# Decoder of two layers: cross attention's last output product in two steps, its last maximum ahead of a division, and steps of five norms set elsewhere in VectorE's order

## The chip, the core and the metric

The kernel runs on one core of one Trainium2 chip. A core has five engines with instruction queues of their own: TensorE (PE, with its weight loads listed apart as PEld), VectorE (DVE), ScalarE (ACT), GpSimd (POOL) and SyncE (SP), which here only starts DMAs. They meet through semaphores. The metric is the device time of one execution in microseconds.

## The reference

The reference takes x (8 sequences of 112 tokens, 512 wide) and a context (8 x 375 x 512) through two pre-norm decoder layers, in float32:

```python
x = x + L0_attn(layernorm(x))                     # 32 query heads, 8 key heads, rotary, sinks
x = x + L0_xattn(layernorm(x), mask, ctx)         # 32 heads of 16; own keys, then gated context keys
x = x + L0_ffn(layernorm(x))                      # router, top 2 of 8 experts, gated GELU
x = x + L1_attn(layernorm(x))                     # causal, 16 query heads, low-rank keys and values
x = x + L1_xattn(layernorm(x), ctx, mask)         # one softmax readout of the context
x = x + L1_ffn(layernorm(x))                      # sigmoid/tanh waves, two blocks with combined weights
```

The masks come with the inputs. `layernorm` takes mean and variance over the 512 channels. In cross attention each head has one softmax over its own 112 keys and another over the 375 context keys; the context's is weighed with tanh of a gate.

## The kernel before

The tokens are 7 tiles of 128 rows (`x`, in SBUF all the time), and the attention stages go by 8 sequences of 112 rows in 4 pairs u. One list of steps, made by `build_order`, is walked by each engine, and each does its own share of a step in that order. A step early in the list is therefore early in every engine's queue that has a share in it, and a wait holds back all that follows on that engine. The functions that make the list merge a chain of attention steps with a row of filling steps: `spread` by costs, `cross` by costs and due times.

A norm of stage st and tile b is three steps. `stats` is VectorE's L1516 to L1520 (mean, variance, plus epsilon) and then GpSimd's power L2251, which gives `rstd`. `scale` is VectorE's L1529, which waits for `rstd`; in stage 0, from tile 4 on, GpSimd's share of `scale` is the addition L2256 of a bias to x. `turn` is TensorE's transposes L1053 and ScalarE's copy L2041. `norms(st, bs)` is all `stats`, then all `scale`.

Layer 0's attention, step by step for a sequence and a half of the heads: `s0` scores (L1100), `m0` maximum on VectorE (L1566) and exponentials on ScalarE, `d0` division on VectorE (L1578 to L1583) and GpSimd (L2271), `p0` transposes (L1109) with copies by ScalarE (even) and VectorE (odd, L1589), `v0` value products (L1119), `w0` output (L1131). The next pair's projections `kq0` (L1080, chunks of 8 matmuls) with their rotary ropes on VectorE (L1549 to L1553) and GpSimd (L2277, L2279) are the filling. A float32 matmul is two records in the trace.

Cross attention handles sequence b in four groups c of eight heads, each with two parities. For the context keys: `xc` scores (L1192), `cm` negative maxima (VectorE, L1634), `mt` turns the maxima on TensorE (L1199) and VectorE adds them to the queries (L1641), so that `xk` (L1209) gives shifted scores, `ce` takes ScalarE's exponentials (L2109), `xcv` is the context value product (L1239). `xu` copies numerator and denominator out of PSUM (ScalarE, L2121). `xd` is the division (VectorE L1649 to the reciprocal L1656; GpSimd L2320, L2325) and `xn` the normed value (L1664, L1666) with event `oxt`. `xw` t is the output product of tile t (L1247), four matmuls over c, and VectorE's addition to x (L1602). Tile 6 needs the last two sequences.

Behind it `ent` steps form the combined weights of layer 1's last stage (L1459, two matmuls of 512 columns each); they have nothing to do with the tokens and fill TensorE's time. Steps 0 to 11 run ahead of the experts. `route` (L1274), `lt` (L1284), VectorE's choice of two experts, `rank` (L1293 to L1296), GpSimd's scattering `put` (L2338), the loading of row blocks, `bt` (L1302) and `gu` (L1312) follow each other.

Layer 1's attention is like layer 0's: `s1`, `c1` 0 (mask addition, VectorE L1842), `c1` 1 (maximum L1848, L1850, and ScalarE's eight exponentials L2161), `p1` (copies L2169 and L1864), `v1` (L1414, copies L2175 and L1870), `w1` (L1426), `d1` (L1856, L1858). GpSimd adds a row to x with `bo1` (L2261).

## Time and profile before

| | us |
|---|---|
| median of 3 runs | 1756.43 |
| lowest and highest | 1752.63, 1756.64 |
| profiled execution, its own time | 1756.78 |
| its span | 1754.5 |
| TensorE busy | 1700.0 (97%) |
| VectorE busy | 986.4 (56%) |
| ScalarE busy | 548.0 (31%) |
| GpSimd busy | 458.5 (26%) |

The span goes from the first to the last recorded instruction; the time of the execution holds some 2.3 us more. The parts of this profile lie at these times: layer 0's attention to about 340 us, cross attention to 901, router and scattering to 946, experts to about 1190, layer 1's attention to about 1480, the readout and the last stage behind it.

### The profile page before, as it was taken

How to read it: one execution, taken by the hardware profiler on the slowest of the kernel's cores; microseconds unless marked ns; L12 is line 12 of the kernel's file. 1: busy time of each engine (PE TensorE's matmuls, PEld its weight loads, DVE VectorE, ACT ScalarE, POOL GpSimd, SP SyncE). 2: the span in 40 equal slices, each digit the busy share in tenths (PEclk: the TensorE clock that was granted, in tenths of full speed). 3: DMA queues.
4: the chain of work that ended last, by engine and by line, in shares of the span. 5: the costliest groups of instructions: out<-in, count | busy, mean ns of one | idle time of the engine just before them, and what ended most of it. 6: DMA issues, size and time to landing. Idle time of an engine off the chain costs nothing.

```text
span 1754.5 us, 32913 instructions
## 1 busy us (share of the span) xinstructions
PE 1700.0 (97%) x13868; PEld 1137.6 (65%) x13868; DVE 986.4 (56%) x1901; ACT 548.0 (31%) x1515; POOL 458.5 (26%) x549
## 2 busy tenths in 40 slices
PE   7999999999999999999999999998999999999998
PEld 6876666657666666666546888877677775444444
DVE  3765556437777777677743111116554555664987
ACT  0343333524444444445410111110422222333411
POOL 2532323512222213222113000005231210002676
PEclk9999999999999999999989999999999999999999
DMA  9100012000000000000147988866000033752101
GB/s 394 49 1 1 1 43 73 1 27 19 13 8 19 4 17 20 8 13 1 67 171 294 347 334 335 335 231 229 2 1 1 1 137 129 241 189 84 29 14 42
DMA packets 31987, 172.26 MB, mean 98 GB/s; under 512 B 4024, under 2 KB 4024, under 8 KB 18176
## 3 DMA queue, kind: packets, MB, share of 16 engines
q1 hardware_dynamic: 29600, 162.82, 24.9%
q0 software_dynamic: 2240, 7.34, 1.2%
q8 instruction: 109, 1.79, 0.4%
q14 instruction: 38, 0.31, 0.1%
HBM read 155.46 MB, written 16.52 MB: 98 GB/s over the span
## 4 chain that ended last, share of the span: by engine, by line
PE 86%; DVE 10%; POOL 1%; issue 1%; ACT 1%; DMA 1%; POOLq 0%; DVEq 0%; ACTq 0%
PE PS L1312 9%; PE PS L1080 7%; PE PS L1131 6%; PE PS L1381 5%; PE PS L1459 5%; PE PS L1169 5%; PE PS L1490 4%; PE PS L1321 4%; PE PS L1426 4%; PE PS L1192 3%; PE PS L1209 3%; PE PS L1477 3%; PE PS L1139 3%; PE PS L1156 2%; PE PS L1161 2%; DVE R L1618 2%
## 5 line engine op out<-in xcount | busy, mean ns | idle before, releaser
L1312 PEld LDWEIGHTS PS<-R,W 128*128 128x128 f32 x1344 | 153.2, 192 | 11.7 <-issue 11.7
L1312 PE MATMUL PS<-R,W 128*128 128x128 f32 x1344 | 153.6, 275 | 2.2 <-DVE R L1811 2.2
L1634 DVE TENSOR_REDUCE nmw<-PS 112x2 f32<-112x750 f32 x128 | 114.1, 934 | 42.5 <-PE PS L1192 42.5
L2251 POOL TENSOR_TENSOR rstd<-veps,mhalf 128x1 f32<-128x1 f32 (+1 forms) x71 | 53.8, 757 | 307.2 <-DVE veps L1520 284.0
L1080 PE MATMUL PS<-xT,W 128*128 128x224 f32 x640 | 127.8, 360 | 1.0 <-ACT xT L2041 0.7
L1080 PEld LDWEIGHTS PS<-xT,W 128*128 128x128 f32 x640 | 122.2, 194 | 9.9 <-issue 7.6
L1818 DVE TENSOR_TENSOR R<-R,PS 128x512 f32<-128x512 f32 x21 | 14.5, 688 | 199.1 <-PE PS L1312 199.1
L1459 PE MATMUL PS<-W 128*128 128x512 f32 x256 | 119.8, 611 | 0.9 <-ACT R L2109 0.9
L2109 ACT ACTIVATE R<-PS 125x672 f32<-125x672 f32 x128 | 86.6, 730 | 85.8 <-PE PS L1209 85.8
L2277 POOL TENSOR_TENSOR R<-R 128x224 f32<-128x224 f32 x80 | 52.8, 661 | 223.4 <-DVE R L1545 116.6
L1381 PE MATMUL PS<-xT,W 128*128 128x224 f32 x512 | 101.9, 359 | 2.5 <-DVE R L1545 2.2
L1490 PE MATMUL PS<-W,xT 128*128 128x512 f32 x224 | 100.7, 593 | 0.9 <-ACT xT L2046 0.9
L1381 PEld LDWEIGHTS PS<-xT,W 128*128 128x128 f32 x512 | 97.2, 193 | 5.1 <-DVE R L1545 2.5
L1131 PE MATMUL PS<-W,R 128*32 128x512 f32 (+1 forms) x512 | 99.1, 594 | 0.0
L2057 ACT ACTIVATE R<-PS,small 112x112 f32<-112x112 f32 x256 | 87.0, 386 | 34.0 <-DVE small L1569 34.0
L1602 DVE TENSOR_TENSOR x<-x,PS 128x512 f32<-128x512 f32 x35 | 24.1, 687 | 120.0 <-PE PS L1131 69.2
L1459 PEld LDWEIGHTS PS<-W 128*128 128x128 f32 x256 | 48.7, 195 | 55.5 <-issue 52.6
L2347 POOL DMA_INDIRECT R<-ys_rows,R x14 | 13.4, 958 | 245.9 <-DMA ys_rows<-R 241.6
L2271 POOL TENSOR_TENSOR R<-R,small 112x448 f32<-112x448 f32 x32 | 42.8, 1336 | 132.0 <-DVE small L1580 132.0
L1426 PE MATMUL PS<-W,R 128*32 128x512 f32 (+1 forms) x384 | 74.8, 594 | 0.7 <-DVE R L1870 0.7
L1321 PE MATMUL PS<-W,R 128*128 128x512 f32 x168 | 75.4, 592 | 0.0
L1131 PEld LDWEIGHTS PS<-W,R 128*32 128x32 f32 (+1 forms) x512 | 35.7, 130 | 60.9 <-issue 60.9
(306 smaller groups left out, 3325.3 us busy)
## 6 DMA issues: line engine op xcount, KB each, us to landing
W<-in_we SPq DMA_DIRECT2D x63, 1024.0 KB, 8.0
R<-in_ctxT SPq DMA_DIRECT2D x12, 750.0 KB, 7.3
W<-in_entwT SPq DMA_DIRECT2D x8, 1024.0 KB, 7.0
W<-in_entpw SPq DMA_DIRECT2D x8, 1024.0 KB, 8.3
R<-in_ctx SPq DMA_DIRECT2D x8, 750.0 KB
xs_rows<-in_x SPq DMA_DIRECT2D x3, 1792.0 KB, 36.1
R<-xs_rows SPq DMA_DIRECT2D x21, 256.0 KB, 8.3
ys_rows<-R SPq DMA_DIRECT2D x21, 256.0 KB, 8.5
```

Source lines behind the costliest of these rows:

```text
L1080: o = e.matmul(PS[:, m, ab * UT:(ab + 1) * UT], lw, xT[:, k, tok], start=k == 0, stop=k == 3)
L1131: o = e.matmul(PS[to, m, :], OT[:, g, c, of], Wo[:, g * 8 + c, :], start=c == 0, stop=c == 7)
L1169: o = e.matmul(PS[0:KC, m, 0:256], CT[b % 2][:, k, t * KC:(t + 1) * KC], Wx[2][:, k, 256 * g:256 * g + 256], start=k == 0, stop=k == 3)
L1312: o = e.matmul(PS[:, m, c * 128:(c + 1) * 128], gate_up(j % 3, k, off + c * 128), BT[:, j % 2, k, :], start=k == 0, stop=k == 3)
L1321: o = e.matmul(PS[:, m, :], GA[:, j % 2, k, :], W[:, GROUPS[j % 3][2], k * D:(k + 1) * D], start=k == 0, stop=k == 3)
L1381: o = e.matmul(PS[:, m, ab * UT:(ab + 1) * UT], Wlq[c // 2][:, c % 2, k, ab * 128:ab * 128 + 128], xT[:, k, tok], start=k == 0, stop=k == 3)
L1426: o = e.matmul(PS[to, m, :], LOT[:, g, c, of], Wlo[2 * g + c // 3][:, c % 3, :], start=c == 0, stop=c == 5)
L1459: o = e.matmul(PS[:, m, :], W[:, wt, kk * D + m * 128:kk * D + (m + 1) * 128], W[:, pw, kk * D:(kk + 1) * D], start=k in starts, stop=k + ...
L1490: o = e.matmul(PS[:, m, :], xT[:, k, tcol(t)], wk[:, k, :], start=k == 0, stop=k == 3)
L1634: e.tensor_reduce(nmw[0:S, par, :].rearrange("p (r f) -> p r f", r=4)[:, r:r + 2, 16 - 16 * par], PS[0:S, r:r + 2, 0:SC], AX.X, ALU.max, n ...
L2057: e.activation(SS[0:S, z, k * S:k * S + S], PS[0:S, r, bcol(j)], ACT.Exp, bias=sm[:, 1, k:k + 1], accum_out=sm[:, 4, k:k + 1])
L2109: e.activation(p_of(b, c, par)[0:KC, r:r + 2, :], PS[0:KC, r:r + 2, 0:3 * S], ACT.Exp).then_inc(*up("cexp", (b, c, par, r)))
```

## The change

Six edits. All but the third only reorder steps.

1. Layer 0, tiles 4, 5 and 6: the `scale` steps, with GpSimd's bias additions, no longer follow their `stats`. One comes behind the first chunk of filling that follows, the other behind the second.
2. Cross attention, last group: `mt` of parity 1 comes ahead of the division `xd` of the group before.
3. `xw` 6 is issued as three matmuls and then one; the first three wait for group 2 of the last sequence, and the fourth for group 3.
4. Two of the four `ent` steps that stood ahead of or around `xw` 6 move behind `rank`. The scale of tile 5 moves from inside the last division to behind the addition of `xw` 6.
5. GpSimd's power in `lt` comes ahead of eight memsets.
6. Layer 1, pair 1: the norm of tile 6 moves from behind the first `s1` to behind the first `c1` 1. (`pace1` gives norm steps no cost; they had none.)

```diff
-        out += runs[n]
+        final = n == 16 * NBATCH - 1
+        out += runs[n][:-1] + [("mt", *pieces_of(n // 4), 1)] + runs[n][-1:] if final else runs[n]
...
-        if n % 4 == 3:
+        if n % 4 == 3 and not final:
             some.insert(1, ("mt", *pieces_of(n // 4), 1))
...
-    at_end = {("xk", 7, 3, 1): h[:1], ("xcv", 7, 3, 1): h[1:4], ("xd", 7, 3): [("scale", 2, 5)], ("xw", 6): h[4:5] + [("turn", 2, 5)] + h[5:6] + [("route", 1)]}
+    at_end = {("xk", 7, 3, 1): h[:1], ("xcv", 7, 3, 1): h[1:2], ("xw", 6): [("scale", 2, 5)] + h[2:3] + [("turn", 2, 5)] + h[3:4] + [("route", 1)]}
...
-    out = [("load", "front", 3), ("load", "we", 0), ("load", "w1s", 0), ("scale", 2, 6), ("turn", 2, 6), ("route", 2), ("lt",)] + part([3]) + [("rank",)]
-    out += part(range(4, FRONT)) + [("ea", 0, k) for k in range(FRONT)] + [("put", t) for t in range(NT)]
+    out = [("load", "front", 3), ("load", "we", 0), ("load", "w1s", 0), ("scale", 2, 6), ("turn", 2, 6), ("route", 2), ("lt",)] + part([2]) + [("rank",)]
+    out += part(range(3, FRONT)) + [("ea", 0, k) for k in range(FRONT)] + [("put", t) for t in range(NT)]
...
+    if step[0] in ("stats", "scale"):
+        return 0.0
...
-            nxt = norms(0, bs) + nxt[:4] + turns(0, bs) + nxt[4:]
+            nxt = [("stats", 0, b) for b in bs] + nxt[:1] + [("scale", 0, bs[0])] + nxt[1:2] + [("scale", 0, b) for b in bs[1:]] + nxt[2:4] + turns(0, bs) + nxt[4:]
...
-            nxt = norms(3, bs) * (u > 0) + nxt[:5] + turns(3, bs) + nxt[5:]
+            nxt = nxt[:5] + turns(3, bs) + nxt[5:]
...
-        out += spread([s for n in range(2 * (u == 0), 4) for s in attend1(4 * u + n)], nxt, pace1)
+        steps = [s for n in range(2 * (u == 0), 4) for s in attend1(4 * u + n)]
+        if u and u + 2 < NU:
+            k = steps.index(("c1", u, 0, 1)) + 1
+            steps[k:k] = norms(3, bs)
+        out += spread(steps, nxt, pace1)
...
-                for b in (t, t + 1):
-                    w.wait_ge(*at("oxt", (b, 3)))
-                xw_part(t, m, range(4)).then_inc(*up("attended", ("xw", t)))
+                w.wait_ge(*at("oxt", (t, 3)))
+                if t == NT - 1:
+                    w.wait_ge(*at("oxt", (t + 1, 2)))
+                    xw_part(t, m, range(3))
+                w.wait_ge(*at("oxt", (t + 1, 3)))
+                xw_part(t, m, range(3 * (t == NT - 1), 4)).then_inc(*up("attended", ("xw", t)))
...
+                e.tensor_tensor(rt[:, 8, 8:8 + NT], rt[:, 8, 0:NT], mhalf[:, 0:NT], ALU.pow).then_inc(*up("rms", 0))
                 for n in range(8):
                     e.memset(rsl(rt, 9)[:, :, n:n + 1], 8.0 - n).then_inc(*up("rank", n))
-                e.tensor_tensor(rt[:, 8, 8:8 + NT], rt[:, 8, 0:NT], mhalf[:, 0:NT], ALU.pow).then_inc(*up("rms", 0))
```

In the changed kernel the lines of the engines lie 7 to 10 further down. VectorE's order in layer 0 at tiles 4 and 5, before:

```order
L1520 TENSOR_SCALAR veps<-mv 128x1
L1529 TENSOR_SCALAR xn<-x,mv,rstd 128x512 x2
L1589 COPY R<-PS 112x448
L1589 COPY row<-PS 112x448
L1566 TENSOR_REDUCE small<-PS 112x8
```

And after, where the first of the two scales stands 16 rows behind the copies:

```order
L1530 TENSOR_SCALAR veps<-mv 128x1
L1599 COPY R<-PS 112x448
L1599 COPY row<-PS 112x448
L1576 TENSOR_REDUCE small<-PS 112x8
...
L1563 SCALAR_TENSOR_TENSOR R<-PS,col,cst 128x224
L1539 TENSOR_SCALAR xn<-x,mv,rstd 128x512
L1559 SCALAR_TENSOR_TENSOR R<-PS,col,cst 128x224
```

The scale (L1529, now L1539) left its place ahead of the copies of transposed probabilities for one between the ropes of two chunks. VectorE's order at the end of cross attention, before (R<-R,PS 128x112 is the addition of the turned maximum, R<-x,mv,rstd a scale):

```order
L1520 TENSOR_SCALAR veps<-mv 128x1
L1649 TENSOR_SCALAR R<-R,cst 128x224
L1651 SCALAR_TENSOR_TENSOR R<-R,cst 128x224
L1654 STREAM_SHUFFLE R<-R 128x224
L1656 RECIPROCAL R<-R 128x224
L1641 TENSOR_TENSOR R<-R,PS 128x112
...
L1656 RECIPROCAL R<-R 128x224
L1529 TENSOR_SCALAR R<-x,mv,rstd 128x512
L1664 TENSOR_TENSOR R<-R 128x224
L1666 SCALAR_TENSOR_TENSOR R<-R,tg 128x112
L1602 TENSOR_TENSOR x<-x,PS 128x512
```

And after:

```order
L1530 TENSOR_SCALAR veps<-mv 128x1
L1651 TENSOR_TENSOR R<-R,PS 128x112
L1659 TENSOR_SCALAR R<-R,cst 128x224
L1661 SCALAR_TENSOR_TENSOR R<-R,cst 128x224
L1664 STREAM_SHUFFLE R<-R 128x224
L1666 RECIPROCAL R<-R 128x224
...
L1666 RECIPROCAL R<-R 128x224
L1674 TENSOR_TENSOR R<-R 128x224
L1676 SCALAR_TENSOR_TENSOR R<-R,tg 128x112
L1612 TENSOR_TENSOR x<-x,PS 128x512
L1539 TENSOR_SCALAR R<-x,mv,rstd 128x512
```

The addition went ahead of the division, and the scale behind the addition of xw 6. VectorE's order in layer 1 at tile 6's norm, before:

```order
L1516 BN_STATS st<-x 128x6
L1518 BN_AGGR mv<-st 128x2
L1520 TENSOR_SCALAR veps<-mv 128x1
L1529 TENSOR_SCALAR xn<-x,mv,rstd 128x512
L1842 TENSOR_TENSOR R<-PS,cst 112x896
L1864 COPY R<-PS 112x448
L1848 TENSOR_REDUCE ls<-R 112x8
L1850 TENSOR_SCALAR ls<-ls 112x8
L1602 TENSOR_TENSOR x<-x,PS 128x512
```

And after:

```order
L1852 TENSOR_TENSOR R<-PS,cst 112x896
L1874 COPY R<-PS 112x448
L1858 TENSOR_REDUCE ls<-R 112x8
L1860 TENSOR_SCALAR ls<-ls 112x8
L1526 BN_STATS st<-x 128x6
L1528 BN_AGGR mv<-st 128x2
L1530 TENSOR_SCALAR veps<-mv 128x1
L1539 TENSOR_SCALAR xn<-x,mv,rstd 128x512
L1612 TENSOR_TENSOR x<-x,PS 128x512
```

The four steps of the norm moved behind mask addition, copy and maximum.

## Rows read from the trace of the kernel before

**Rows 1.** The page: busy us, share and instructions; the chain by engine.
```profile
PE 1700.0 (97%) x13868; PEld 1137.6 (65%) x13868; DVE 986.4 (56%) x1901; ACT 548.0 (31%) x1515; POOL 458.5 (26%) x549
PE 86%; DVE 10%; POOL 1%; issue 1%; ACT 1%; DMA 1%; POOLq 0%; DVEq 0%; ACTq 0%
```
**Rows 2.** Timeline, layer 0: start us, us, engine, line, out<-in, xcount, [idle before <-releaser].
```profile
71.82 0.96 PE L1119 MATMUL PS<-R 112*64 112x448 f32 x2
71.96 1.26 POOL L2256 TENSOR_TENSOR x<-x,row 128x512 f32<-128x512 f32 x1
72.09 1.41 DVE L1529 TENSOR_SCALAR xn<-x,mv,rstd 128x512 f32<-128x512 f32 x1 [0.52 <-POOL rstd L2251]
73.42 0.61 DVE L1589 COPY R<-PS 112x448 f32<-112x448 f32 x1
74.09 0.97 PE L1119 MATMUL PS<-R 112*64 112x448 f32 x4 [1.30 <-DVE R L1589]
75.74 8.59 PE L1080 MATMUL PS<-xT,W 128*128 128x224 f32 x44
...
88.43 1.34 PE L1119 MATMUL PS<-R 112*64 112x448 f32 x5
90.08 3.29 PE L1080 MATMUL PS<-xT,W 128*128 128x224 f32 x16
```
**Rows 3.** Timeline, layer 0, TensorE at tile 6's norm.
```profile
114.94 2.07 PE L1119 MATMUL PS<-R 112*64 112x448 f32 x6
117.69 7.13 PE L1131 MATMUL PS<-W,R 128*128 128x512 f32 x16
```
**Rows 4.** Timeline, cross attention's last group, TensorE and VectorE.
```profile
882.02 0.32 PE L1199 MATMUL PS<-cst,nmw 112*128 112x112 f32 x1
883.45 1.55 DVE L1656 RECIPROCAL R<-R 128x224 f32<-128x224 f32 x1
884.92 0.21 DVE L1641 TENSOR_TENSOR R<-R,PS 128x112 f32<-128x112 f32 x1
885.18 0.92 PE L1209 MATMUL PS<-R 32*125 32x112 f32 x24 [0.82 <-DVE R L1641]
886.98 3.78 PE L1459 MATMUL PS<-W 128*128 128x512 f32 x4 [0.88 <-ACT R L2109]
```
**Rows 5.** Windows: stretch, length, busy us (instructions) by engine, PEclk, DMA share, GB/s.
```profile
882.00:886.00 4.00, 2.45 (x69) 1.77 (x65) 3.68 (x10) 1.35 (x2) 2.17 (x3) 1.00 0.25 104
886.20:893.00 6.80, 6.02 (x30) 2.64 (x31) 0.32 (x1) 1.89 (x3) 0.00 (x0) 0.50 0.01 4
...
910.20:913.50 3.30, 3.30 (x5) 1.25 (x4) 2.81 (x14) 0.05 (x1) 0.00 (x0) 0.50 1.01 425
```
**Rows 6.** Timeline, the last division, the last output product and behind it.
```profile
892.11 0.54 ACT L2121 ACTIVATE R<-PS 128x448 f32<-128x448 f32 x1 [4.56 <-PE PS L1239]
895.46 0.45 DVE L1529 TENSOR_SCALAR R<-x,mv,rstd 128x512 f32<-128x512 f32 x1
896.24 0.34 DVE L1666 SCALAR_TENSOR_TENSOR R<-R,tg 128x112 f32<-128x112 f32 x1
897.75 3.60 PE L1247 MATMUL PS<-W,R 128*128 128x512 f32 x8
901.18 1.88 PE L1459 MATMUL PS<-W 128*128 128x512 f32 x4
```
**Rows 7.** Timeline, TensorE's weight loads at the first block of the experts.
```profile
944.25 0.42 PEld L1302 LDWEIGHTS PS<-cst,R 128*128 128x128 f32 x4 [0.84 <-DMA R<-xs_rows]
```
**Rows 8.** Timeline, layer 1, around tile 6's norm.
```profile
1294.31 4.95 POOL L2261 TENSOR_TENSOR x<-x,R 128x512 f32<-128x512 f32 x4
1299.87 0.55 DVE L1529 TENSOR_SCALAR xn<-x,mv,rstd 128x512 f32<-128x512 f32 x1 [5.34 <-POOL rstd L2251]
1302.00 0.78 PE L1414 MATMUL PS<-R 112*32 112x112 f32 x24 [1.12 <-DVE R L1864]
1306.65 1.02 PE L1346 MATMUL PS<-W,xT 128*112 128x96 f32 x8 [1.25 <-ACT R L2175]
```

## Prediction

> **What bounds the kernel now.** I read the page first: its busy line and its chain of waits [rows 1]. TensorE is busy for 1700.0 of 1754.5 us and carries 86% of the chain. So a microsecond is saved only where TensorE stands still or runs slowly, and work of another engine counts only where TensorE waits for it. The page cannot say where the missing 54.5 us lie, so I went through TensorE's timeline stretch by stretch, looking for idle time in brackets and for steps that last longer than the same step elsewhere. Three stretches lie where the change moves something: the value products of layer 0 near 72 and 115 us [rows 2, 3], the end of cross attention between 882 and 902 us [rows 4, 6], and a step near 1300 us in layer 1 [rows 8]. Last I read the granted clock around them [rows 5].
>
> A caution for reading: TensorE's ends are modelled, so a row with a long duration may hide a wait. Where I can I measure from start to start, against the same step where nothing is late.
>
> **Part 1, layer 0's norms (tiles 4 and 5, and tile 6).** `scale` is L1529 on VectorE. At tiles 4 and 5 VectorE runs it twice, the second time in 1.41 us, and only then the copies L1589 that the value product L1119 waits for [rows 2]. From the start of L1119 at 71.82 to the next projection at 75.74 are 3.92 us. The same products take 1.65 us (88.43 to 90.08) where nothing is late. The stall is 3.92 - 1.65 = 2.27 us. Without the scales the first copy can start about where the first scale stood, near 71.0 us, and two copies of 0.61 us end near 72.3, when TensorE asks for them. I count all 2.27 us. At tile 6 the stretch from 114.94 to 117.69 is 2.75 us, so 2.75 - 1.65 = 1.10 us [rows 3]. Together 3.37 us.
>
> What the moved steps cost in their new places: each scale (0.55 us where it runs alone [rows 8]) now stands between the ropes of two projection chunks. A chunk is 16 records and takes TensorE about 3.1 us [rows 2], and VectorE is busy only 56% of the time [rows 1], so it has room. GpSimd's addition L2256 (1.26 us) goes with each scale and now stands behind the rope of one chunk, ahead of the next rope or of the normalization of probabilities; no DMA moves, and SyncE's queue is the same. TensorE's next transposes need GpSimd's half of the probabilities. I set 0.1 us against the gain, with ends of 0 and 0.9 us for each of three scales. The upper end is the nearest row: the scale that ran beside GpSimd's addition took 1.41 instead of 0.55 us [rows 2, 8], 0.86 us more.
> Of that row the Trainium skill (SBUF — State Buffer, "SBUF: two separate sides") gives a reason: VectorE in its faster modes and GpSimd share a pair of ports under an exclusive lock, and the loser is blocked for the whole instruction. The trace agrees: that scale ended at 73.50, 0.28 us after the addition that began at 71.96. The rule speaks against this change, which puts scales among GpSimd's ropes; its price is a rival below.
>
> **Part 2, the last maximum ahead of the division.** TensorE waits 0.82 us at 885.18 for L1641, which adds the turned maximum [rows 4]. TensorE had turned it at 882.02. VectorE however ran the division first, up to the reciprocal of 1.55 us at 883.45, and reached L1641 only at 884.92. Put ahead, L1641 (0.21 us) ends near 882.7, before TensorE asks for it (885.18 - 0.82 = 884.36). The 0.82 us go. The division starts some 0.3 us later; it feeds the output of the product before last, and xw 6 asks for that some 8 us on. TensorE's wait for ScalarE's exponentials at 886.98, 0.88 us, has another cause and stays.
>
> **Part 3, the last output product in two steps, and two steps of the combined weights behind it.** Before, TensorE has three `ent` steps between the last context product and xw 6 (L1247 at 897.75) [rows 6]. Beside them runs the chain to the last normed value: ScalarE's copy at 892.11, VectorE's division, a scale at 895.46, then L1666 that ends at 896.24 + 0.34 = 896.58. These are 4.47 us, of which the scale takes some 0.4, so about 4.1 us without it. Xw 6 takes 3.43 us (897.75 to 901.18) for 8 records, 0.43 us each; an `ent` step has four records of the same width, 1.72 us. Cover after the change: one `ent` (1.72) and three quarters of xw 6 (2.57), 4.29 us. Cover and chain nearly meet: I take a new wait of 0.1 us, ends 0 and 0.5 us. The other two `ent` steps are not removed; TensorE does them behind `rank`, and their 3.44 us gain nothing of their own. They give reserve later: TensorE's weight load for the experts' first block stood idle for 0.84 us until its rows had landed [rows 7]. `rank` and all that follows from it on GpSimd and SyncE now come 3.44 us earlier measured in TensorE's work. I count 0.3 us (ends 0 and 0.6, since part of such idle time lies under the matmul before). The scale of tile 5 now stands behind the addition of xw 6 and delays the last tile's statistics by its 0.45 us; two `ent` steps, a turn and `route` on TensorE cover that. The power ahead of the memsets on GpSimd I cost at nothing: TensorE's `lt`, which gives the logits, ends later than both.
>
> **The clock around it.** From 886.2 to 893.0 us the granted clock is 0.50, that is 1.2 instead of 2.4 GHz, and in the 4 us ahead of it TensorE was busy for 2.45 us [rows 5]. The 6.02 us of work done at half clock would take 3.0 us at full. The change takes 0.82 us of the waits out, and behind the wait at 886.98 it adds none worth the name. I think it likelier that the fall is shortened or does not come: a gain of 1.5 us (half of the stretch back) to 3.0 us, and I take 2.2 us. That nothing comes back is a rival. The fall from 910.2 to 913.5 [rows 5] follows work that the change leaves alone and stays.
> The Trainium skill (TensorE: Matmul & The Clock Gate, "What's actually happening") says that the default is the slow clock, that activity releases it, and that the outcome varies from run to run with the phase of the monitor at the start. No run here shows that; by it either outcome of this term may be had from the same program.
>
> **Part 4, layer 1.** The norm's L1529 waits 5.34 us for `rstd`, since GpSimd is in four additions of `bo1` (4.95 us from 1294.31) [rows 8]. VectorE's mask addition, copy and maximum for the next attention step queue behind it. TensorE waits 1.12 us for the copy L1864 at 1302.00, and 1.25 us at 1306.65 for ScalarE's L2175, which queues behind eight exponentials that were late for the same reason. With the norm behind the maximum these run while TensorE is still in w1's product. Both waits go: 1.12 + 1.25 = 2.37, say 2.4 us, with ends of 2.0 and 2.9 (in part 1 the stall was 1 us more than its bracket of 1.30 us). The scale still ends near 1300.4, and the turn that needs it comes behind w1, `td`, `vp1` and `ku`. The addition of w1's product waits behind the scale for some 0.3 us, and nobody waits for it.
>
> **The sum.** 2.27 + 1.10 - 0.1 + 0.82 - 0.1 + 0.3 + 2.2 + 2.4 = 8.9 us. The profiled execution took 1756.78 us (span 1754.5), 0.35 us above the median of 1756.43. Against the one that makes 1747.9, against the other 1747.5. I say **1747.5 us**, 0.5% faster.
>
> **The rivals.**
> The clock falls as before (chance 0.24): two waits for ScalarE remain in that stretch, and they may be enough. Then 8.9 - 2.2 = 6.7 us are gained: 1749.7 us.
> Scales and additions collide (0.11), as the lock of ports would have it: each of three scales lasts 0.86 us longer and TensorE's transposes wait for it. 2.6 us less, and the clock's gain halved: 8.9 - 2.6 - 1.1 = 5.2 us, 1751.2 us.
> The gain comes back (0.14): TensorE's 54.5 us of idle time are many small waits, so there are many engines just ahead of it that would now be just behind it, and half of the gain is lost: 1752. Against it speaks that no other engine is busy for more than 56% of the span [rows 1].
> Slower (0.04), one mechanism: TensorE stops ahead of the last quarter of xw 6, the clock falls to 0.50 there and stays, and all work from there to the end of `rank` is done at half clock. At full clock that work is an estimated 15 us (xw 6's 3.43, four `ent` steps of 1.72, and some 5 for turns, `route`, `lt` and `rank`). It would cost up to 15 us and give up to 1762.5. It decides from 9 us of additional half-clock work on; the two falls of [rows 5] had 6.0 and 3.3 us of it.
> Otherwise (0.47) my forecast, between 1743.5 and 1750.5.
>
> **How the numbers follow.** 0.3% of 1756.43, 5.3 us, is about what a measurement of this kernel can tell from no change; the border is 1751.2. Faster: 0.47, most of 0.24 and a little of the two next, 0.73 in all. Same: 0.23. Slower: 0.04. The lower end of the range takes in all of the clock's gain, every cost at nothing and the upper ends of parts 3 and 4, and the timed runs of before, which lie 4 us apart: 1743. The upper end takes in all rivals but the slow one, with half a microsecond: 1752.5.
>
> **What would show it.** Right: no idle time ahead of L1119 in the first two places; the maximum's addition ahead of the division and no wait of the last xk product; xw 6 in two pieces with under 0.5 us between them; neither wait in the layer 1 step; less time at clock 0.50 near 886. Wrong: a scale of over 1 us between ropes with TensorE waiting behind it; a fall of the clock at xw 6; or the same sum of idle time for TensorE in other places.

## The result, and the profile after

The changed kernel takes 1747.32 us (median of 4 runs, 1745.11 to 1747.57) beside 1756.54 for the kernel before (4 runs, 1752.63 to 1757.42): ratio 0.9949, 95% interval 0.9932 to 0.9966. A second comparison gave 1747.05 beside 1756.83, ratio 0.9947, 0.9931 to 0.9964. It is faster by half a per cent, and the first median is 0.2 us from the forecast of 1747.5. The profiled execution took 1747.09 us with a span of 1745.1, 9.4 us less than the span before.

The busy line, from the page of the changed kernel; it answers to [rows 1]:

```profile
PE 1694.6 (97%) x13868; PEld 1135.8 (65%) x13868; DVE 987.2 (57%) x1901; ACT 548.5 (31%) x1515; POOL 459.0 (26%) x549
```

The number of instructions is the same to the last one. TensorE's busy time fell by 5.4 us with 13868 matmuls in both, and its idle time by 4.0. That is no division into clock and waits: the clock is worth 2.8 us in this pair, as worked out below, and the rest of the 5.4 us are waits that the modelled ends of the matmuls count as busy. So I compared TensorE's timeline place by place, from the start of a step to the start of the next.

**Layer 0.** The timeline of TensorE in the changed kernel at the first of the two places of [rows 2], and at the place of [rows 3] (start us, us, engine, line):

```profile
71.47 1.34 PE L1126 MATMUL PS<-R 112*64 112x448 f32 x5
...
73.12 3.10 PE L1087 MATMUL PS<-xT,W 128*128 128x224 f32 x15
...
112.95 1.34 PE L1126 MATMUL PS<-R 112*64 112x448 f32 x5
...
114.60 1.98 PE L1138 MATMUL PS<-W,R 128*128 128x512 f32 x4
```

From 71.47 to 73.12 and from 112.95 to 114.60 are 1.65 us each, where before they were 3.92 and 2.75. Both stalls are gone whole: 2.27 and 1.10 us, as summed. What I had set at 0.1 us against them is larger. All engines of the changed kernel where tile 5's scale now stands:

```profile
79.40 1.27 POOL L2266 TENSOR_TENSOR x<-x,row 128x512 f32<-128x512 f32 x1
...
81.59 0.80 DVE L1593 TENSOR_TENSOR R<-R,small 112x448 f32<-112x448 f32 x1
81.87 1.77 POOL L2281 TENSOR_TENSOR R<-R,small 112x448 f32<-112x448 f32 x1
82.31 0.54 DVE L1539 TENSOR_SCALAR xn<-x,mv,rstd 128x512 f32<-128x512 f32 x1
83.79 0.95 PE L1116 MATMUL PS<-cst,R 112*112 112x112 f32 x8 [0.55 <-POOL R L2281]
```

TensorE waits for GpSimd's half of the probabilities (L2281). It starts late, behind tile 4's bias addition (L2266) and two ropes, and it lasts 1.77 us with the scale beside it. From the start of these transposes (L1116, 82.31) to the scores behind them (84.67) are 2.36 us, where 1.74 us are the time without a wait (84.92 to 86.66 before): 0.62 us are lost.

**The end of cross attention.** VectorE in the changed kernel, where [rows 4 and 6] were, and TensorE beside it:

```profile
881.09 0.27 DVE L1651 TENSOR_TENSOR R<-R,PS 128x112 f32<-128x112 f32 x1 [0.15 <-PE PS L1206]
...
882.58 1.55 DVE L1666 RECIPROCAL R<-R 128x224 f32<-128x224 f32 x1
...
891.54 0.34 DVE L1676 SCALAR_TENSOR_TENSOR R<-R,tg 128x112 f32<-128x112 f32 x1
```
```profile
883.01 0.92 PE L1216 MATMUL PS<-R 32*125 32x112 f32 x24
884.81 1.98 PE L1469 MATMUL PS<-W 128*128 128x512 f32 x4 [0.88 <-ACT R L2119]
...
889.26 3.80 PE L1254 MATMUL PS<-W,R 128*128 128x512 f32 x8
892.90 1.88 PE L1469 MATMUL PS<-W 128*128 128x512 f32 x4
```

The addition L1651 stands ahead of the division and L1216 waits for nothing: 0.82 us forecast, 0.89 read between the landmarks. The wait of 0.88 us for the exponentials stays, but the `ent` step behind it takes 1.98 instead of 3.78 us. Xw 6 takes 3.64 us (889.26 to 892.90) instead of 3.43: a wait of 0.21 us ahead of its last quarter, for the value that was ready at 891.88.

**The clock.** Windows of the changed kernel (stretch, length, busy us and instructions of PE, PEld, DVE, ACT, POOL; then the granted clock, DMA share, GB/s):

```profile
745.00:749.90 4.90, 4.90 (x40) 2.45 (x40) 2.65 (x5) 1.06 (x2) 1.33 (x2) 0.65 0.01 3
886.20:893.00 6.80, 6.80 (x39) 2.95 (x38) 3.47 (x7) 0.54 (x1) 1.59 (x2) 1.00 0.00 0
910.20:913.50 3.30, 3.30 (x9) 1.44 (x8) 2.89 (x15) 0.00 (x0) 2.35 (x3) 1.00 0.21 79
1213.40:1216.60 3.20, 3.20 (x10) 2.88 (x10) 3.13 (x6) 0.00 (x0) 2.04 (x3) 0.50 0.04 15
```

Both falls of [rows 5] are missing; a new one stands at 745, and one near 1213 has its like in the profile before, near 1221. Measured from start to start, the first absent fall gave 2.88 us (10.77 us from 886.98 to xw 6 before, now 4.45 and two moved `ent` steps of 1.72), the second 1.49, and the new one took 1.58.

**Layer 1.** TensorE before, at the two ends of the step of [rows 8]:

```profile
1294.84 5.33 PE L1426 MATMUL PS<-W,R 128*128 128x512 f32 x12
...
1309.31 0.66 PE L1053 MATMUL PS<-cst,xn 128*128 128x128 f32 x4
```

And the whole of it in the changed kernel:

```profile
1288.20 5.33 PE L1436 MATMUL PS<-W,R 128*128 128x512 f32 x12
1293.46 1.36 PE L1424 MATMUL PS<-R 112*32 112x112 f32 x48
1294.75 1.73 PE L1340 MATMUL PS<-xT,W 128*64 128x224 f32 x8
1296.41 1.81 PE L1356 MATMUL PS<-W,xT 128*112 128x96 f32 x16
1298.15 1.78 PE L1348 MATMUL PS<-R,W 64*128 64x224 f32 x8
1299.86 0.66 PE L1060 MATMUL PS<-cst,xn 128*128 128x128 f32 x4
```

Neither wait is left. From the start of w1's product (L1436) to the turn (L1060) are 11.66 us; before, it was 14.47 us. The gain is 2.81 us; 2.4 were forecast.

The ledger of the traced pair: layer 0 -3.37 and +0.62; the maximum -0.89; clock -2.88 - 1.49 + 1.58; xw 6 +0.21; layer 1 -2.81: -9.0 us. With small differences at the start, near 380 us, in `rank` and in the experts (under 0.4 each) it comes to -9.4.

### The profile page after: what moved, and what is told of

Read it like the earlier page. It is cut to its first block, busy times and chain, and to the rows that moved or that the text cites. A ratio compares the mean times of both kernels' runs of the same rounds, so it can differ in the third digit from the quotient of the medians.

```text
span 1745.1 us, 32913 instructions
## 1 busy us (share of the span) xinstructions
PE 1694.6 (97%) x13868; PEld 1135.8 (65%) x13868; DVE 987.2 (57%) x1901; ACT 548.5 (31%) x1515; POOL 459.0 (26%) x549
## 4 chain that ended last, share of the span: by engine, by line
PE 86%; DVE 9%; POOL 2%; issue 1%; ACT 1%; DMA 1%; POOLq 0%; DVEq 0%; ACTq 0%
PE PS L1322 9%; PE PS L1087 6%; PE PS L1138 6%; PE PS L1391 5%; PE PS L1469 5%; PE PS L1176 5%; PE PS L1500 4%; PE PS L1436 4%; PE PS L1331 4%; PE PS L1199 3%; PE PS L1216 3%; PE PS L1487 3%; PE PS L1146 3%; PE PS L1163 2%; PE PS L1168 2%; DVE R L1628 2%
## 5 line engine op out<-in xcount | busy, mean ns | idle before, releaser
L1469 PE MATMUL PS<-W 128*128 128x512 f32 x256 | 115.8, 594 | 0.9 <-ACT R L2119 0.9
L2281 POOL TENSOR_TENSOR R<-R,small 112x448 f32<-112x448 f32 x32 | 43.2, 1351 | 132.9 <-DVE small L1590 132.9
L1436 PE MATMUL PS<-W,R 128*32 128x512 f32 (+1 forms) x384 | 74.8, 594 | 0.7 <-DVE R L1880 0.7
```

The lines of the kernel that those rows point to most:

```text
L1436: o = e.matmul(PS[to, m, :], LOT[:, g, c, of], Wlo[2 * g + c // 3][:, c % 3, :], start=c == 0, stop=c == 5)
L1469: o = e.matmul(PS[:, m, :], W[:, wt, kk * D + m * 128:kk * D + (m + 1) * 128], W[:, pw, kk * D:(kk + 1) * D], start=k in starts, stop=k + ...
```

## The experiments

Two questions were open: is each gain that of its own edit, and how much of the result is the clock, which may fall differently in the next execution? A single profile shows local waits well. For the clock I use the mean granted clock of every execution. The clock's cost is the span times one minus that mean, since work at 0.50 takes twice as long. This is somewhat too high, as waits in such a stretch cost nothing more: the three stretches above would be 3.4, 1.7 and 1.7 us by it, and were 2.88, 1.49 and 1.58. The mean is rounded to 0.001, which is 1.75 us, so only averages over several executions are used.

**Edit 1 alone** (kernel before, layer 0's scales set apart):

```diff
-            nxt = norms(0, bs) + nxt[:4] + turns(0, bs) + nxt[4:]
+            nxt = [("stats", 0, b) for b in bs] + nxt[:1] + [("scale", 0, bs[0])] + nxt[1:2] + [("scale", 0, b) for b in bs[1:]] + nxt[2:4] + turns(0, bs) + nxt[4:]
```

> The kernel before with the first edit alone (scales of layer 0's tiles 4, 5 and 6 set apart from their statistics). Theory (the edit's worth is the stall of the value products less a collision of scale and additions on VectorE and GpSimd): from the first value product near 71.8 us to the first projection 1.65 instead of 3.92 us, at tile 6 1.65 instead of 2.75 us, and a new wait of about 0.6 us at the next transposes, 3.37 - 0.6 = 2.8 us in all by 340 us of the span. Rival (the lock of ports makes every moved scale 0.86 us longer): at least two of the three scales take over 1.3 us and less than 1.5 us is gained. Rival (the gain comes back): under 1.5 us is left at the first product of cross attention. The later falls of the clock, near 886, 910 and 1220 us, should then stand as in the kernel before if they are tied to the work.

Measured 1751.66 us beside 1757.0, span 1749.9 (one execution each). Both stretches of value products last 1.65 us, and the new wait is there: 2.8 us in all from start to start, as expected. TensorE, edit 1 alone:

```profile
83.04 0.95 PE L1109 MATMUL PS<-cst,R 112*112 112x112 f32 x8 [0.52 <-POOL R L2271]
...
881.34 0.92 PE L1209 MATMUL PS<-R 32*125 32x112 f32 x24 [0.82 <-DVE R L1641]
883.14 1.98 PE L1459 MATMUL PS<-W 128*128 128x512 f32 x4 [0.88 <-ACT R L2109]
```

So gain and cost in layer 0 are both edit 1's own. The last two rows show more: the waits of [rows 4], 0.82 and 0.88 us, are both present, with the old code, and the clock stayed at full speed (1.98 us, not 3.78). The waits alone do not decide the fall. The fall near 910 is missing too, and one that the profile of before does not have stands at 1301, for 6.8 us, in the old code of layer 1.

**Edit 2 alone** (kernel before, `mt` 7 3 1 ahead of `xd` 7 2), one execution and then ten:

```diff
-        out += runs[n]
+        final = n == 16 * NBATCH - 1
+        out += runs[n][:-1] + [("mt", *pieces_of(n // 4), 1)] + runs[n][-1:] if final else runs[n]
...
-        if n % 4 == 3:
+        if n % 4 == 3 and not final:
```

> The kernel before with the second edit alone (the last turned maximum is added ahead of the division). Theory: the wait of 0.82 us at the last shifted product goes, and as the three output steps and everything else stay, any further change there is the clock's. If one wait less is enough to keep the clock, the stretch near 886 us runs at 1.00 and 3 us more are gained, 3.8 us in all; if the clock falls because of the waits for ScalarE that remain, only 0.8 us, with half clock for 3 to 7 us. Nothing before 880 us moves; the fall near 746 us that the changed kernel showed should appear here as often as in the kernel before if it is a matter of the single execution.

> The kernel before with edit 2 alone, as in the version only max, now in several executions, to count the clock. Seven executions of the kernel before had a mean granted clock of 0.993 to 0.996 (mean 0.995). Theory A (edit 2 keeps the clock up): the mean over these executions rises to 0.997, and the time falls by 0.9 us of waits and some 3 us of clock: median 1753. Theory B (edit 2 is worth its wait alone, and the clock's falls come from all stretches with short waits together): mean clock 0.995 to 0.996, median 1755.5 to 1756.

The first took 1752.16 us (span 1750.4), and its clock held behind the wait for the exponentials (the `ent` step took 1.98 us). The ten later ones took 1753.26 (median, 1751.62 to 1756.91) beside 1757.13 (15 executions), ratio 0.9978, 0.9969 to 0.9987. The mean clock over the ten is 0.9962, beside 0.9947 for the 15 of the kernel before. That is 2.7 us less of clock cost and 1.0 us of the rest: one reordered VectorE instruction of 0.21 us is worth 3.7 us, not 0.9. Theory A of the second text holds in size, though the mean clock lies a little under its 0.997. But it is no switch; TensorE of the profile of those ten:

```profile
883.95 0.92 PE L1210 MATMUL PS<-R 32*125 32x112 f32 x24
885.75 3.64 PE L1460 MATMUL PS<-W 128*128 128x512 f32 x4 [0.88 <-ACT R L2110]
```

The 0.82 us are gone and the clock fell at the next wait all the same (3.64 us).

**Edit 6 alone** (kernel before, layer 1's norm behind the maximum):

```diff
-            nxt = norms(3, bs) * (u > 0) + nxt[:5] + turns(3, bs) + nxt[5:]
+            nxt = nxt[:5] + turns(3, bs) + nxt[5:]
...
+        if u and u + 2 < NU:
+            k = steps.index(("c1", u, 0, 1)) + 1
+            steps[k:k] = norms(3, bs)
...
```

> The kernel before with the sixth edit alone (layer 1, the norm of tile 6 behind the maximum). Theory: both waits there (1.12 and 1.25 us) go and 2.8 us are gained from the second value product to the rotary keys' product; the scale ends ahead of TensorE's turn. Rival (the wait moves on to w1's addition or to the turn): under 1.5 us. The falls of the clock near 886 and 910 us are untouched by this edit and should both be there if they come from the waits ahead of them; if one is missing, it depends on the execution.

Measured 1750.51 us, span 1748.5. TensorE, edit 6 alone:

```profile
1291.56 5.33 PE L1432 MATMUL PS<-W,R 128*128 128x512 f32 x12
...
1303.22 0.66 PE L1059 MATMUL PS<-cst,xn 128*128 128x128 f32 x4
```

From 1291.56 to 1303.22 are 11.66 us, as in the changed kernel: the 2.81 us are this edit's. The rest of the 6 us of span is not. The fall near 886 is missing here as well, with cross attention as it was before, and so is the one near 1221; one of 6.8 us stands at 906.

**Edits 3 to 5 alone** (kernel before, with the last output product split, the two `ent` steps behind `rank`, and the power ahead of the memsets):

```diff
-    at_end = {("xk", 7, 3, 1): h[:1], ("xcv", 7, 3, 1): h[1:4], ("xd", 7, 3): [("scale", 2, 5)], ("xw", 6): h[4:5] + [("turn", 2, 5)] + h[5:6] + [("route", 1)]}
+    at_end = {("xk", 7, 3, 1): h[:1], ("xcv", 7, 3, 1): h[1:2], ("xw", 6): [("scale", 2, 5)] + h[2:3] + [("turn", 2, 5)] + h[3:4] + [("route", 1)]}
...
```

> The kernel before with edits 3, 4 and 5 (output product in two steps, two steps of combined weights behind rank, power ahead of memsets), without the maximum ahead of the division. Theory: the wait of 0.82 us at the last shifted product stays, the clock falls near 886 us as before (0.50 for one or two stretches, 1.5 to 3.4 us lost), and the two moved steps give about 0.3 us at the experts' first block: at most 1 us faster than before by the first experts' product, if nothing changes elsewhere. Rival (it is the shorter path to the router that brought the gain): over 2.5 us faster at the experts' first product.

Measured 1759.67 us beside 1756.83, one execution with a mean clock of 0.993, the lowest of any profile here. TensorE, from the last xk product to xw 6:

```profile
886.37 0.92 PE L1209 MATMUL PS<-R 32*125 32x112 f32 x24 [0.81 <-DVE R L1644]
888.17 3.66 PE L1462 MATMUL PS<-W 128*128 128x512 f32 x4 [0.88 <-ACT R L2112]
...
894.29 3.80 PE L1247 MATMUL PS<-W,R 128*128 128x512 f32 x8
897.93 1.88 PE L1462 MATMUL PS<-W 128*128 128x512 f32 x4
```

Xw 6 takes 3.64 us, as in the changed kernel. From 888.17 to the experts' first product at 947.49 are 59.3 us, before 58.9 (886.98 to 945.90), with the same half-clock time in both. These edits bring nothing by themselves; whether they also draw more falls of the clock one execution cannot say.

**The changed kernel without the split** (xw 6 waits for the last value and is done whole):

```diff
-                w.wait_ge(*at("oxt", (t, 3)))
-                if t == NT - 1:
-                    w.wait_ge(*at("oxt", (t + 1, 2)))
-                    xw_part(t, m, range(3))
-                w.wait_ge(*at("oxt", (t + 1, 3)))
-                xw_part(t, m, range(3 * (t == NT - 1), 4)).then_inc(*up("attended", ("xw", t)))
+                for b in (t, t + 1):
+                    w.wait_ge(*at("oxt", (b, 3)))
+                xw_part(t, m, range(4)).then_inc(*up("attended", ("xw", t)))
```

> The changed kernel without the third edit: the last output product waits for all four groups before its first matmul. Theory (cover meets chain): the chain from ScalarE's copy to the last normed value is about 4.1 us and one step of the combined weights covers 1.7 us, so TensorE waits 2.3 to 2.6 us ahead of the last output product and the output product takes 3.4 us, where the changed kernel has 3.64 us for it: 2.2 to 2.4 us more in that place. It also tests the clock: with a wait of over 2 us there, the granted clock should fall behind it to 0.50, costing up to 1.7 us or more in the products that follow. Rival (the split is worth nothing, since the chain is shorter than believed): under 0.5 us.

Measured 1748.99 us, span 1746.6. TensorE, and the window behind the wait:

```profile
889.13 5.40 PE L1254 MATMUL PS<-W,R 128*128 128x512 f32 x8 [2.51 <-DVE R L1673]
894.37 1.88 PE L1466 MATMUL PS<-W 128*128 128x512 f32 x4
```
```profile
890.20:893.40 3.20, 3.20 (x5) 1.22 (x4) 0.00 (x0) 0.00 (x0) 0.00 (x0) 0.50 0.00 0
```

The chain from ScalarE's copy to the last value is nearly as long as the prediction had it (4.29 us for 4.1): with one `ent` step and no split, 2.51 us of it stand open. Xw 6 then runs at half clock, 5.24 us. This is the slow rival in small: in this one profile a fall of 3.4 us stands right behind the wait, and another of 3.4 us at 904, but the clock does not stay down to the end of `rank`.

**The changed kernel without edit 2** (all else changed):

```diff
-        final = n == 16 * NBATCH - 1
-        out += runs[n][:-1] + [("mt", *pieces_of(n // 4), 1)] + runs[n][-1:] if final else runs[n]
+        out += runs[n]
...
-        if n % 4 == 3 and not final:
+        if n % 4 == 3:
```

> The changed kernel without edit 2: the division again ahead of the maximum's addition, everything else changed. Idle time: 0.82 us of waiting for the addition come back near 882, +0.9 us. Theory A (the maximum's place also kept the clock from falling): the mean granted clock over the executions, 0.997 in seven of eight executions of the changed kernel, goes back by 0.001 to 0.002 in most of them, a fall near 886 is seen in about half of the profiles, and the median is 1749.5 to 1750.5. Theory B (the falls at this place came by chance, and edit 2 is worth its wait alone): mean clock 0.997 in most executions, no more half-clock time than the changed kernel, median 1748.0.

Measured 1748.45 us (4 runs: 1750.96, 1745.55, 1750.88, 1746.02), ratio 0.9945, 0.9930 to 0.9960. The executions are of two kinds: spans 1743.6 twice with a mean clock of 0.998, and 1748.7 and 1748.9 with 0.995. Less the clock's cost all four come to 1740.0 to 1740.2. The profile is of the second kind and has the fall at the known place (TensorE; 0.82 us are back):

```profile
883.78 0.92 PE L1215 MATMUL PS<-R 32*125 32x112 f32 x24 [0.82 <-DVE R L1650]
885.58 3.57 PE L1468 MATMUL PS<-W 128*128 128x512 f32 x4 [0.88 <-ACT R L2118]
```

The median lies between the two theories, and four executions don't separate them from the changed kernel (0.9965 against 0.9969). What these executions do show is that one and the same code differs by 5 us with the clock alone.

**The changed kernel again**, more executions and a second profile:

> The changed kernel once more, unchanged, beside the kernel before: 0.9949 of its time (1747.3 us). Its new trace is what counts: if the fall of the clock at 746 us, which the kernel before did not have, and the absence of the one behind lt belong to the code, both are seen again; if they belong to the execution, at least one differs, by 1.5 to 3 us each.

1747.05 us (4 runs, 1746.07 to 1749.39), span 1744.3. Windows of this second profile:

```profile
745.00:749.90 4.90, 4.90 (x48) 2.77 (x47) 3.54 (x7) 0.88 (x3) 0.89 (x2) 1.00 0.00 0
...
898.30:904.90 6.60, 6.60 (x15) 3.73 (x15) 3.11 (x15) 0.25 (x1) 0.00 (x0) 0.50 0.92 386
1213.40:1216.60 3.20, 2.82 (x15) 2.82 (x16) 3.16 (x6) 0.00 (x0) 2.04 (x3) 1.00 0.03 10
```

The falls at 745 and 1213 are gone and one at 898, inside `lt`, is there: the same code, other places. Local waits are the same to 0.01 us (0.55 us near 83).

**The changed kernel shifted** by some 1.5 us of extra work on TensorE near 236 us (the transposes of cross attention's first turn four times, to the same end):

```diff
-                for c in range(4):
+                for c in [n % 4 for n in range(16 if (st_, b) == (1, 0) else 4)]:
```

> The changed kernel with twelve more transposes of 0.11 us in the first turn of cross attention (the same transposes four times over), which shifts everything behind 225 us by some 1.3 us and nothing else; results are the same. It tests whether the clock's falls belong to the waits alone. If they do, the trace equals that of the changed kernel but for 1.3 us, with the falls near 746 and 1216 us in the same places of the program. If the monitor's phase decides, a fall comes or goes: near 746, 886, 901 to 905 or 1213 us, 1.5 to 3 us each.

1747.11 us, span 1745.3. All waits stand at their places (0.54 us near 84, ahead of the shift), and the only half-clock stretch in mid-kernel is at 1214. The shift brought no additional fall. Since the unshifted kernel has different falls from one profile to the next, one profile cannot say whether the shift took any away.

**More norms set apart**, on top of the change: tile 5's scale one chunk later, and the scales of tiles 0 and 1 in layer 0's last unit apart as well.

```diff
-            nxt = [("stats", 0, b) for b in bs] + nxt[:1] + [("scale", 0, bs[0])] + nxt[1:2] + [("scale", 0, b) for b in bs[1:]] + nxt[2:4] + turns(0, bs) + nxt[4:]
+            nxt = [("stats", 0, b) for b in bs] + nxt[:1] + [("scale", 0, bs[0])] + nxt[1:3] + [("scale", 0, b) for b in bs[1:]] + nxt[3:4] + turns(0, bs) + nxt[4:]
...
-            nxt = norms(1, (0, 1)) + nxt[:4] + turns(1, (0, 1)) + norms(1, (2,)) + nxt[4:] + turns(1, (2,))
+            nxt = [("stats", 1, 0), ("stats", 1, 1)] + nxt[:1] + [("scale", 1, 0)] + nxt[1:2] + [("scale", 1, 1)] + nxt[2:4] + turns(1, (0, 1)) + norms(1, (2,)) + nxt[4:] + turns(1, (2,))
```

> The changed kernel with two more placements: tile 5's scale stands one chunk later (behind kq0 1 4), and the scales of cross attention's first two norms, tiles 0 and 1, are set apart from their statistics in the same way (behind the first and second chunk of the last pair). Theory: the wait of 0.55 us for GpSimd at the transposes near 84 us goes, and the stall of 2.3 us of the value products near 202 us (1.38 us in brackets) goes too: 2.5 to 2.8 us faster than the changed kernel, 1744.7 us. Rival (collisions of scales with GpSimd): a new wait of 0.5 us or more at the transposes that follow, under 1.7 us gained.

1745.44 us (4 runs, 1745.15 to 1746.60), ratio 0.9936, 0.9919 to 0.9952. GpSimd, then TensorE:

```profile
81.01 1.31 POOL L2281 TENSOR_TENSOR R<-R,small 112x448 f32<-112x448 f32 x1
...
89.99 1.83 POOL L2281 TENSOR_TENSOR R<-R,small 112x448 f32<-112x448 f32 x1 [6.08 <-DVE small L1590]
```
```profile
91.17 0.63 PE L1060 MATMUL PS<-cst,xn 128*128 128x128 f32 x4 [0.67 <-DVE xn L1539]
...
199.22 1.78 PE L1126 MATMUL PS<-R 112*64 112x448 f32 x6
...
201.68 7.13 PE L1138 MATMUL PS<-W,R 128*128 128x512 f32 x16
```

Without the scale beside it GpSimd's normalization takes 1.31 instead of 1.77 us, and of the 0.62 us near 83 only 0.16 are left (the transposes and what follows them start 1.90 us apart, for 1.74): the scale made 0.46 us of them, GpSimd's late start the rest. But the scale now stands beside the next normalization, which takes 1.83 us, and tile 5's turn waits 0.67 us for it. From the first places of edit 1 to 112 us TensorE loses 1.24 us this way, where the changed kernel loses 0.62. The gain comes from the second edit: the stretch from 199.22 lasts 2.46 us. In the changed kernel (second profile) it takes 4.00, the old stall of scales ahead of copies:

```profile
198.93 0.97 PE L1126 MATMUL PS<-R 112*64 112x448 f32 x2
...
202.93 7.13 PE L1138 MATMUL PS<-W,R 128*128 128x512 f32 x16
```

**Only the second of these edits** (the last line pair of the diff above):

> The changed kernel with one further edit: the scales of tiles 0 and 1 in layer 0's second round of norms stand one projection chunk apart each; tile 5's scale stays where the change put it (in the version more norms it stood a chunk later as well). In the version more norms the stretch of value products near 199 us fell from 4.00 to 2.46 us, and the wait of 0.55 us near 83 went, but one of 0.67 us for tile 5's scale came at 91.17, and TensorE was 0.29 us later at 112.7 than with the changed kernel. Theory (each scale costs by its own place, and the moves are independent): the wait of 0.55 us near 83 is back, no wait near 91, the stretch near 199 lasts 2.46 us, and the span is 1.5 us below the changed kernel's and some 0.3 us below more norms's: a median of 1745.5, ratio to before 0.9934. Rival (the gain near 199 needs both moves, or is given back before 380 us): 1747.0, as the changed kernel.

1743.75 us (5 runs, 1742.32 to 1745.79), ratio 0.9922, 0.9909 to 0.9936: the lowest median of all versions, though its interval overlaps that of the version before it. The wait of 0.54 us near 83 is back, none stands near 91, and the stretch near 199 takes 2.46 us: the moves are independent, as the theory had it. The median is 1.75 us under the 1745.5 forecast, and more than half of that is clock (4.2 us of cost beside 5.2 and 5.7 of the changed kernel, below). TensorE there, and later, in the same profile:

```profile
198.81 1.79 PE L1126 MATMUL PS<-R 112*64 112x448 f32 x6
...
201.27 7.13 PE L1138 MATMUL PS<-W,R 128*128 128x512 f32 x16
...
880.78 3.68 PE L1469 MATMUL PS<-W 128*128 128x512 f32 x4 [0.88 <-ACT R L2119]
```

The last row is a fall of the clock at the place where edit 2 was to prevent it, in the one execution of the five (0.996; the other four 0.998) that was profiled.

**All executions together** (spans in us; the clock's cost is worked out as said above; the two rows of before are those beside the second and the third set of runs; the four means of the first row of the changed kernel all read 0.997, so that its rounding does not average out):

| kernel | executions | mean span | mean clock | clock's cost | the rest |
|---|---|---|---|---|---|
| before | 7 | 1755.0 | 0.9950 | 8.8 | 1746.2 |
| before | 15 | 1755.4 | 0.9947 | 9.4 | 1746.0 |
| changed | 4 | 1744.7 | 0.9970 | 5.2 | 1739.5 |
| changed, again | 4 | 1745.5 | 0.9968 | 5.7 | 1739.8 |
| edit 2 alone | 10 | 1751.7 | 0.9962 | 6.7 | 1745.0 |
| changed without edit 2 | 4 | 1746.2 | 0.9965 | 6.1 | 1740.1 |
| more norms apart | 4 | 1743.6 | 0.9975 | 4.4 | 1739.3 |
| only the second of these | 5 | 1742.1 | 0.9976 | 4.2 | 1737.9 |

And by place of the fall, over the thirteen profiles (one of each version, the changed kernel twice): at the wait for the last exponentials, near 885, it is seen in 3 of 5 without edit 2 and in 2 of 8 with it; in the layer 1 step near 1300 in 3 of 5 without edit 6 and in 0 of 8 with it. But for the one at 890 behind the wait of 2.51 us, all falls in mid-kernel stand at five places: these two, between 898 and 914 in 9 of 13 profiles, between 1211 and 1225 in 6, and near 745 in 4. The place that is hit most is in and behind `lt`, where TensorE has waits of 0.78 and 0.48 us in every version.

## Why the prediction was right

**The sum without the clock was 8.9 - 2.2 = 6.7 us; the table gives 6.2 to 6.7**, according to which rows are set against each other. The edits add up, place by place and from start to start: edit 1 alone gives 2.8 us, edit 2 0.9, edit 6 2.8, and edits 3 to 5 cost 0.2, 6.3 together; the changed kernel shows 6.2. The rival in which the gain comes back is thereby excluded. Whole spans of single executions do not serve for such a sum: the same product near 66 us, ahead of all that the edits touch, starts between 65.0 and 66.6 us in the thirteen profiles, and in that of before at 66.5, among the latest.

**Luck.** That the median of the first comparison is 0.2 us from the forecast is in part luck: its four executions lie 2.5 us apart, and the second comparison gave a gain of 9.8 us where the first gave 9.2. The errors of the terms also cancel: costs of 0.5 (part 1) and 0.1 us (part 3) and a gain of 0.2 us (the experts) were missed on one side, 0.4 us of layer 1 and about 1 us of clock on the other.

**Part 1.** The stalls were right to 0.01 us (2.27 and 1.10). The term of 0.1 us against them was the mis-sized one: it measured 0.62. The two ends I had set (0 and 0.9) held it, and the cause was the one named, a scale beside GpSimd's work, but at another step. I had looked for a scale of over 1 us; the scale kept its 0.54 us, and GpSimd's normalization was the one stretched, from 1.31 to 1.77 us, with and without the scale beside it.
By the Trainium skill (SBUF — State Buffer, "SBUF: two separate sides") the one of VectorE and GpSimd that starts first has the shared ports for its whole instruction, and the other is blocked. The trace agrees in that VectorE's product L1593 (81.59) starts ahead of GpSimd's L2281 (81.87), and GpSimd is the one held up. But the scale starts at 82.31, behind GpSimd's, and still keeps its 0.54 us; that differs from the rule, and the trace decides: GpSimd had to wait for both of VectorE's instructions. L2281 ends 0.79 us after the last of them here, 0.79 us with L1593 alone beside it (80.72 to 81.53, L2281 to 82.32 in more norms), and takes 0.93 us where VectorE has neither beside it (333.18 in the changed kernel). I should have charged the lock to whichever of the two TensorE asks for next, and for as long as VectorE goes on without a pause.

**Part 2.** The wait went (0.82 forecast, 0.89 read). The wait for the exponentials stayed, as said.

**Part 3.** A new wait of 0.1 us was forecast, 0.21 measured, well inside the ends; the chain took 4.30 us (887.58 to 891.88) for 4.1, and the version without the split confirms it. The 0.3 us counted for the experts was too much. The idle weight load of [rows 7] is gone, but from the start of the four matmuls there to the next product are 1.59 us now (937.85 to 939.44) and were 1.65 before: the idle time lay under the matmul ahead, and the row was worth 0.06 us. Both errors are small, and the edits 3 to 5 brought nothing to be measured.

**The clock.** I said 2.2 us, with ends of 1.5 and 3.0, at the fall behind 886; the traced pair gives 2.88 there. Over all executions and places the clock gave 3.1 us beside the second set of the kernel before, and 3.1 to 4.2 over all pairs of rows. So the sign was right and the size too small: between 2.6 (3.1 less 15%, the most by which the reckoning was too high above) and 4.2 us. And "the clock falls as before" is not what happened. Two steps of the working were wrong. "The fall from 910.2 to 913.5 stays": the code there is unchanged, and still it was absent in the changed kernel's first profile, and in the second one stands at 898 instead. Whether a fall comes at such a place is a draw of the single execution, with odds that belong to the place (9 of 13 here). And the clock's gain is not all edit 2's: it is worth 2.7 us where made alone, while without it the changed kernel still has 0.9965. The falls near 1300, seen in 3 of 5 profiles without edit 6 and in none of 8 with it, suggest that taking out the two layer 1 waits pays in clock as well. That was not measured over many executions and stays open, as does the reason why one execution falls at a place and the next does not.
The Trainium skill (TensorE: Matmul & The Clock Gate, "What's actually happening") says, of the first matmuls of a kernel, that the outcome varies from run to run. Runs of this case show the like in mid-kernel: 1743.6 and 1748.9 us of span from the same program.

**Part 4.** 2.81 us for a forecast of 2.4 with ends of 2.0 and 2.9. The brackets of the two waits add to 2.37; start to start gives 0.44 more, as the prediction's own caution about modelled ends would have had it. For part 1 I measured from start to start, here I added brackets.

**The slow rival** needed TensorE to stop ahead of the last quarter and the clock to stay down. The stop was 0.21 us, and xw 6 ran at full clock in both profiles of the changed kernel; the fall at 898 in the second one begins 7.5 us behind it. Even a stop of 2.51 us had 3.4 us of half clock right behind it and 6.8 us up to `rank`, under the 9 us that the rival needed.

## What to carry to other kernels

Read a stall from the start of a step to the start of the next, against the same step where nothing is late; the stalls read so came out within 0.1 us here, while brackets and idle weight loads were off by 0.4 and 0.2. When a VectorE step is moved, look at what GpSimd does beside its new place and who waits for that. Compare two profiles from a landmark ahead of the change, not from the start of the span. Treat clock falls of one profile as draws: count them by the mean clock of many executions. A wait of 0.82 us taken out of a cluster of short waits gave some 2.7 us of clock here.

## What the runs showed of the hardware

- The same program has its half-clock stretches at other places from one execution to the next: 745 and 1213 us in one profile of the changed kernel, only 898 to 905 in the other. The kernel before shows mean clocks from 0.993 to 0.996 in 22 executions, and its span goes with them, from 1753.1 to 1756.8 us.
- The same two waits (0.82 and 0.88 us) stood ahead of a half-clock stretch of 6.8 us in the profile of before and of none with edit 1 alone.
- GpSimd's normalization of 112x448 (L2281) took 0.93 us with neither of VectorE's two instructions beside it, 1.31 to 1.37 beside VectorE's half of it (L1593), and 1.77 and 1.83 where a scale followed L1593 without a pause. In the 31 cases of the changed kernel that had L1593 beside it, it ended 0.78 to 0.80 us after the last of these two, and the scale itself kept 0.54 us. In [rows 2], where GpSimd's addition came first, it was the scale that was stretched, to 1.41.
